# A two-layer graph network on one core: ACT fetches three of its edge tiles per sixteen bodies instead of one, between its scalings

## The reference, cut to what matters

```
hid    = silu(edge_scalars @ fc1)              # 10 or 64 inputs per edge
weight = hid @ fc2                             # 192 or 224 factors
row    = h[edge_src]                           # 160 numbers of the source node
msg    = weight * row, times parts of edge_attr (4 numbers)
agg    = segment_sum(msg, edge_dst)            # edges are sorted by destination
```

## Time and profile before

| | |
|---|---|
| median of 3 runs | 4053.01 us (4050.89 to 4054.45) |
| the profiled execution | 4054.16 us, its span 4052.2 us |
| PE busy | 3404.4 us (84%) |
| POOL busy | 2982.6 us (74%) |
| ACT busy | 2569.3 us (63%) |
| DVE busy | 2477.8 us (61%) |
| row fetches issued by SP / by ACT | 6208 / 1536 |
| granted clock of PE, mean | 0.99 |

### The profile page before, as it was taken

The page is one execution under the profiler, slowest core; times in us unless marked ns, Lnnn a source line. Parts: engine busy times, 40 slices in busy tenths (PEclk is TensorE's granted clock), DMA queues, the critical chain, the costliest instruction groups (busy, mean ns, idle before and its releaser), DMA issues. The chain is left out here.

```text
span 4052.2 us, 253752 instructions
## 1 busy us (share of the span) xinstructions
PE 3404.4 (84%) x91120; PEld 2590.9 (64%) x91121; DVE 2477.8 (61%) x7032; ACT 2569.3 (63%) x10506; POOL 2982.6 (74%) x3211
## 2 busy tenths in 40 slices
PE   8888888888887888888888888888888888888887
PEld 6666666666655665666776666666666666666666
DVE  6555555555545545445567777777776666666667
ACT  6666666666666666666466666666666666666665
POOL 5777777777777777777457777777777777777775
PEclk9999999999999999999999999999999999999999
DMA  5333333333333333333244444444443333333334
GB/s 158 86 86 88 86 88 88 87 86 86 81 75 76 78 75 76 77 76 76 84 130 112 109 112 109 109 112 110 111 113 100 97 100 100 97 100 99 97 100 122
DMA packets 357221, 390.23 MB, mean 96 GB/s; under 512 B 155141, under 2 KB 278825, under 8 KB 356646
## 3 DMA queue, kind: packets, MB, share of 16 engines
q0 software_dynamic: 147168, 251.36, 25.3%
q10 hardware_dynamic: 94848, 72.93, 6.7%
q1 hardware_dynamic: 114728, 61.70, 5.6%
HBM read 357.01 MB, written 23.76 MB: 94 GB/s over the span
## 5 line engine op out<-in xcount | busy, mean ns | idle before, releaser
L655 POOL DMA_INDIRECT e_rows<-scratch_table,k_index x3066 | 2899.7, 946 | 976.3 <-issue 831.3
L716 ACT ACTIVATE e_match<-e_match,e_attr 128x40 f32<-128x40 f32 x9408 | 2138.8, 315 | 36.5 <-issue 35.5
L773 PE MATMUL e_sum<-e_match,e_msg 128*32 128x40 f32 (+1 forms) x81536 | 1549.2, 215 | 513.4 <-DVE e_msg L986 248.0
L773 PEld LDWEIGHTS e_sum<-e_match,e_msg 128*32 128x32 f32 x81536 | 1340.1, 111 | 886.5 <-DVE e_msg L989 370.0
L980 DVE TENSOR_TENSOR e_msg<-e_w,e_rows 128x512 f32<-128x512 f32 x790 | 543.2, 688 | 1446.1 <-DMA e_rows<-scratch_table,k_index 1402.5
L707 ACT ACTIVATE e_hidden<-e_h 100x512 f32<-100x512 f32 (+1 forms) x784 | 384.2, 490 | 1329.4 <-PE e_h L755 1290.9
L766 PEld LDWEIGHTS e_w<-k_fc,e_hidden 100*128 100x128 f32 (+1 forms) x6272 | 808.7, 189 | 348.2 <-issue 330.2
L766 PE MATMUL e_w<-k_fc,e_hidden 100*128 100x192 f32 (+1 forms) x6272 | 1025.6, 366 | 0.6 <-issue 0.3
L755 PE MATMUL e_h<-e_inputs,k_fc 128*100 128x512 f32 (+1 forms) x1568 | 711.7, 536 | 105.0 <-issue 61.3
L986 DVE TENSOR_TENSOR e_msg<-e_w,e_rows 128x384 f32<-128x384 f32 x790 | 430.7, 545 | 0.3 <-issue 0.2
L983 DVE TENSOR_TENSOR e_msg<-e_w,e_rows 128x384 f32<-128x384 f32 x790 | 430.4, 545 | 0.0
(11 more groups left out here) (131 smaller groups left out, 1027.5 us busy)
## 6 DMA issues: line engine op xcount, KB each, us to landing
e_kept_rows<-scratch_table SPq DMA_DIRECT2D x6208, 0.6 KB
e_inputs<-in_inputs ACTq DMA_DIRECT2D x196, 256.0 KB
e_rows<-scratch_table,k_index POOLq DMA_INDIRECT x3066, 2.8
e_act_rows<-scratch_table ACTq DMA_DIRECT2D x1536, 0.6 KB
e_attr<-in_edge_attr ACTq DMA_DIRECT2D x390, 24.0 KB
e_inputs<-in_inputs ACTq DMA_DIRECT2D x196, 40.0 KB
e_xb<-in_xT SPq DMA_DIRECT2D x50, 128.0 KB
scratch_yT<-m_yT SPq DMA_DIRECT2D x10, 640.0 KB, 4.1
```

The source lines that it names most:

```text
L655: pool.indirect_dma_start(out=rows[j][:, t, :], out_offset=None, in_=table_dram, in_offset=bass.IndirectOffsetOnAxis(ap=index[k][:, c:c + ...
L716: last = nc.scalar.activation(match[j][:, t, c, :], match[j][:, t, 4, :], ACT.Copy, scale=attr[q][:, e0 + t, e:e + 1])
L773: return nc.tensor.matmul(out[32 * g:32 * g + 32, c0:c0 + n, :], m[:, f:f + 32], m5[:, which:which + n, :], start=first and opens, stop=en ...
```

## The change

ACT now fetches three tiles per span: group 2 at positions 5, 10 and 15. POOL leaves out the last tile of these three groups. SP's part stays as it is. ACT's 128 rows of a tile are spread evenly over the groups from the one two after the last placed tile to the one before the next (22, 18 and 18 groups), and within a group over four portions, one after the three scalings of each tile. A register load stands before every eighth row, wherever that falls. The copy into `rows` stands after the scalings of the group, and the load of the next node numbers right behind it.

```diff
--- before.py
+++ after.py
-FETCHED, FETCHED_GROUP, ACT_GROUP = (3, 7, 11, 15), 1, 2
+FETCHED, FETCHED_GROUP = (3, 7, 11, 15), 1
+ACT_FETCHED, ACT_GROUP = (5, 10, 15), 2
...
+def act_rows_due(position, j):
+
+    g = GPB * position + j
+    for k, at in enumerate(ACT_FETCHED):
+        first = GPB * ACT_FETCHED[k - 1] + ACT_GROUP + 2 if k else 0
+        count = GPB * at + ACT_GROUP - first
+        if first <= g < first + count:
+            return k, P * (g - first) // count, P * (g - first + 1) // count
+    return 0, 0, 0
...
-                fetched = started and (position in FETCHED and j == FETCHED_GROUP or position == SPAN - 1 and j == ACT_GROUP)
+                fetched = started and (position in FETCHED and j == FETCHED_GROUP or position in ACT_FETCHED and j == ACT_GROUP)
...
-            def row_numbers(span, batch):
+            def row_numbers(span, k, batch):
                 if batch == 0:
-                    landed, free = 16 * (span + 1), 16 * (FIRST + SPAN * span)
+                    landed = 16 * (len(ACT_FETCHED) * span + k + 1)
+                    free = 16 * (FIRST + SPAN * span + (ACT_FETCHED[k - 1] + 1 if k else 0))
...
-            def fetch_rows(batch, numbers, first, last):
-                for r in range(first, last):
-                    p = batch * BATCH + r
-                    act.dma_start(act_rows[p:p + 1, :], table_dram[bass.ds(numbers[r], 1), :]).then_inc(act_row_in, 16)
-
-            def place_rows(span):
-                landed, summed = 16 * P * (span + 1), GPB * (FIRST + SPAN * span + SPAN - 2) + ACT_GROUP + 1
+            def rows_between(span, position, j, loaded):
+
+
+                k, begin, end = act_rows_due(position, j)
+                shares = [range(begin + (end - begin) * t // TPG, begin + (end - begin) * (t + 1) // TPG) for t in range(TPG)]
+
+                def fetch(t):
+                    for p in shares[t]:
+                        if p % BATCH == 0:
+                            loaded[:] = row_numbers(span, k, p // BATCH)
+                        act.dma_start(act_rows[p:p + 1, :], table_dram[bass.ds(loaded[p % BATCH], 1), :]).then_inc(act_row_in, 16)
+                return fetch
+
+            def place_rows(span, k):
+                landed = 16 * P * (len(ACT_FETCHED) * span + k + 1)
+                summed = GPB * (FIRST + SPAN * span + ACT_FETCHED[k] - 1) + ACT_GROUP + 1
...
-                last.then_inc(scaled, 1)
+                    if t == TPG - 1:
+                        last.then_inc(scaled, 1)
+                    fetch(t)
...
                 for position in range(SPAN):
-                    each = BATCH // 2 if position == SPAN - 1 else BATCH // GPB
                     for j in range(GPB):
-                        places = position == SPAN - 1 and j == ACT_GROUP
-                        scale_matches(FIRST + SPAN * span + position, j, places)
-                        if j == 0:
-                            numbers = row_numbers(span, position)
-                        fetch_rows(position, numbers, min(j * each, BATCH), min(j * each + each, BATCH))
+                        places = position in ACT_FETCHED and j == ACT_GROUP
+                        fetch = rows_between(span, position, j, loaded)
+                        scale_matches(FIRST + SPAN * span + position, j, fetch, places)
                         if places:
-                            place_rows(span)
-                load_act_index(span + 1)
+                            k = ACT_FETCHED.index(position)
+                            place_rows(span, k)
+                            load_act_index(len(ACT_FETCHED) * span + k + 1)
```

More of the change, by code:

```diff
@@ L60 @@
 PER_BODY = 4
-FETCHED, FETCHED_GROUP, ACT_GROUP = (3, 7, 11, 15), 1, 2
+FETCHED, FETCHED_GROUP = (3, 7, 11, 15), 1
+ACT_FETCHED, ACT_GROUP = (5, 10, 15), 2
 PER_TILE = P // BATCH
 assert FIRST + SPAN * SPANS == BODIES and (NT - FIRST) % SPAN == 0 and SPAN == 4 * FETCHED[0] + 4
-assert PER_BODY * SPAN == len(FETCHED) * PER_TILE and SPAN == PER_TILE
+assert PER_BODY * SPAN == len(FETCHED) * PER_TILE and SPAN == ACT_FETCHED[-1] + 1
 FETCHED_TILES = SPANS * len(FETCHED)
@@ L70, in fetched_tile, with act_tile @@
     return ((FIRST + which * PER_BODY + PER_BODY - 1) * GPB + FETCHED_GROUP) * TPG + TPG - 1
-def act_tile(span):
-    return ((FIRST + span * SPAN + SPAN - 1) * GPB + ACT_GROUP) * TPG + TPG - 1
+ACT_TILES = SPANS * len(ACT_FETCHED)
+def act_tile(which):
+    span, k = divmod(which, len(ACT_FETCHED))
+    return ((FIRST + span * SPAN + ACT_FETCHED[k]) * GPB + ACT_GROUP) * TPG + TPG - 1
+def act_rows_due(position, j):
[6 more added lines that the diff above has]
+    return 0, 0, 0
 C_S, C_X = float(np.sin(np.pi / 8)), float(np.cos(np.pi / 8))
@@ L672, in _, with load_act_index @@
         def _(act):
-            def load_act_index(span):
-                act.dma_start(act_index[:, :], d["act_index"][:, bass.ds(span * BATCH, BATCH)]).then_inc(act_index_in, 16)
-            def row_numbers(span, batch):
+            def load_act_index(which):
+                act.dma_start(act_index[:, :], d["act_index"][:, bass.ds(which * BATCH, BATCH)]).then_inc(act_index_in, 16)
+            def row_numbers(span, k, batch):
                 if batch == 0:
-                    landed, free = 16 * (span + 1), 16 * (FIRST + SPAN * span)
+                    landed = 16 * (len(ACT_FETCHED) * span + k + 1)
+                    free = 16 * (FIRST + SPAN * span + (ACT_FETCHED[k - 1] + 1 if k else 0))
                     act.compute_val(landed)
@@ L701, in place_rows, with scale_matches @@
                 act.dma_start(rows[ACT_GROUP][:, TPG - 1, :], act_rows[:, :]).then_inc(act_placed, 16)
-            def scale_matches(i, j, places=False):
+            def scale_matches(i, j, fetch, places=False):
                 g, q, e0 = GPB * i + j, j // 2, (j % 2) * TPG
@@ L729, in _ @@
                 for j in range(GPB):
-                    scale_matches(i, j)
+                    scale_matches(i, j, lambda t: None)
             with act.Fori(0, SPANS) as span:
+                loaded = []
                 for position in range(SPAN):
-                    each = BATCH // 2 if position == SPAN - 1 else BATCH // GPB
                     for j in range(GPB):
-                        places = position == SPAN - 1 and j == ACT_GROUP
-                        scale_matches(FIRST + SPAN * span + position, j, places)
-                        if j == 0:
-                            numbers = row_numbers(span, position)
-                        fetch_rows(position, numbers, min(j * each, BATCH), min(j * each + each, BATCH))
+                        places = position in ACT_FETCHED and j == ACT_GROUP
+                        fetch = rows_between(span, position, j, loaded)
+                        scale_matches(FIRST + SPAN * span + position, j, fetch, places)
                         if places:
-                            place_rows(span)
-                load_act_index(span + 1)
-            act.wait_ge(act_index_in, 16 * (SPANS + 1))
+                            k = ACT_FETCHED.index(position)
+                            place_rows(span, k)
+                            load_act_index(len(ACT_FETCHED) * span + k + 1)
+            act.wait_ge(act_index_in, 16 * (ACT_TILES + 1))
             for q in range(2):
@@ L1359 @@
     ("src", (P, T + 2 * STEP), I32), ("dst_tile", (P, T), I32),
[L1360 removed]
+    ("row_index", (PER_TILE, (FETCHED_TILES + 2) * BATCH), I32), ("act_index", (PER_TILE, (ACT_TILES + 1) * BATCH), I32), ("dst_by_group", (GP, GQ, GE), I32),
     ("edge_attr", (P, T + STEP, 6), F32), ("inputs0", (NB0, EPAD + STEP * P), F32),
@@ L1439, in lay_out @@
     r["row_index"] = r["row_index"].reshape(PER_TILE, -1)
-    r["act_index"] = np.zeros((PER_TILE, SPANS + 1, BATCH), np.int32)
-    for span in range(SPANS):
-        r["act_index"][:, span] = by_tile[act_tile(span)]
+    r["act_index"] = np.zeros((PER_TILE, ACT_TILES + 1, BATCH), np.int32)
+    for which in range(ACT_TILES):
+        r["act_index"][:, which] = by_tile[act_tile(which)]
     r["act_index"] = r["act_index"].reshape(PER_TILE, -1)
```

## The result

The changed kernel takes 4023.52 us (median of 6 runs, 4019.09 to 4025.33), the kernel before 4052.39 us on the same chip (6 runs, 4050.89 to 4054.45): a ratio of 0.9927, 95% interval 0.9914 to 0.9939, 28.9 us less. The profiled execution took 4024.55 us, its span 4022.7 us.

What follows compares the result with a forecast made beforehand. POOL's back-to-back gather issue was taken to bind: 4054.2 us profiled, less 30.0 for 24 gathers, plus 1 for late chains, gives 4025.2; the runs' median lies 1.1 lower, so 4024 us, range 4020 to 4038.

Steps and rivals of the forecast that it cites:

- POOL's pace: POOL's gathers run back to back, 1.2506 us each; 24 fewer save 30.0 us, span 313.90 to 311.4 us.
- That POOL's issue time binds, and not the transfers: DMA engines are busy only 0.39 of the time; gathers come at POOL's own pace, 1.245 us each.
- ACT's part costs nothing: ACT's queue needs 282 us per span, 91% of POOL's 311.4, so its added fetches were taken as 0.
- Even there ACT's 4.8 just fits: In heavy stretches, ACT's 4.8 us per group fits within POOL's 4.86 to 4.93 us.
- The latency reserve: ACT's silu ahead of PE's next hidden product: ACT can be 3.2 us late before PE notices.
- The wait for the last row before the copy: ACT's place instruction waits 0 to 2.8 us for its last fetched row; nothing behind it is lost.
- SP falls behind but doesn't bind: With node terms SP needs 313.3 us per span, falling 1.9 us behind each; its index load has 8.8 us reserve.
- The late chains: SP's late placed tiles delay DVE, PE's sums and then POOL: 0 to 3 us together, 1 us in the sum.
- The first: SP's reserves are missing, so it binds in spans with node terms: 11 us come back, 4035 us; chance 0.12.
- The second: ACT overflows in heavy stretches as register loads wait for queued scalings: with four waited for, 4177 us; chance 0.09.
- Its point of decision: At 0.66 us of waiting per ACT register load, ACT's span reaches 314 us, the time of before.
- The third: No change: ACT and SP together eat the gain, about 4050 us; chance 0.05.

Runs made afterwards that it cites:

- POOL's part alone: Kernel before, with POOL skipping the two more gathers per span and nothing added to ACT (two tiles keep old rows): 4021.52 us, ratio 0.9927; slow chip 0.9948.
- ACT's part alone: Changed kernel, but POOL gathers all tiles as before; ACT fetches three tiles, copies only position 15's: 4050.76 us, ratio 0.9998; slow chip 1.0068.
- few register loads on ACT: Changed kernel, with ACT loading new row numbers only every fourth time, so rows of other edges are fetched: 4023.95 us, ratio 0.9930.
- four tiles: Changed kernel, with ACT fetching four tiles per span, group 2 at positions 3, 7, 11 and 15: 4680.3 us, ratio 1.1548.
- fewer register loads on SP: Changed kernel, with SP loading row numbers once per body instead of every eight rows, so rows of other edges are fetched: 4019.99 us, ratio 0.9921.
- the repeat of the changed kernel: Changed kernel with an unused SP register load that was absent from the program that ran, so the same kernel again: 4024.11 us, ratio 0.9927.
- fetches at the end: Changed kernel, with all of ACT's fetches of a group after its twelve scalings instead of in portions: 4021.03 us, ratio 0.9924; slow chip 1.0018.

## Why the prediction was right

**POOL's pace: right.** 24 gathers at 1.2506 us each were to give 30.0 us; POOL's part alone gave 30.3 us, the span of 16 bodies went to 311.43 us (311.4 predicted), and the 0.305 us before each gather stayed.

**That POOL's issue time binds, and not the transfers: right.** In the kernel with ACT's part alone 3072 rows more are fetched and the time is unchanged. In the one with POOL's part alone 24 gathers fewer give their full pitch. The sentence of the Trainium skill weighed in the prediction ("DMA: Bandwidth & Descriptors", section "Issuing engines are not separate DMA queues"), that the issuing engine's time is usually small beside the DMA, doesn't hold for these gathers: each takes 1.25 us of POOL's queue, where the page of the profile has a median of 2.9 us from issue to landing. A row costs 0.39 us of ACT's queue; its landing time is in no trace.

**ACT's part costs nothing: right, with two sizes off.** A fetch costs 0.39 us as predicted (1168.34 - 1167.95). The base of a group is 3.96 - 7 x 0.39 = 1.23 us, not 1.05. The load and its first fetch cost 5.02 - 3.96 = 1.06 us (1.09 predicted). A heavy group therefore takes 4.95 us on the mean of layer 0, (28 x 5.02 + 4 x 3.96 + 4 x 5.42) / 36, not 4.8; that is over PE's and POOL's 4.86 to 4.93. "Even there ACT's 4.8 just fits" was wrong by 0.15 us a group: ACT falls behind in each heavy stretch. With the light groups at 4.4 us and the empty ones at 3.1 us when ACT is late, it is 22 x 4.4 + 36 x 4.95 + 6 x 3.1 = 294 us per span, 94% of 311.4 instead of 91%.

**The latency reserve: right for PE, and not the last one.** Silu was to be late by at most 3.2 us before PE notices. Behind a heavy group it is late by 2.3 us in the median and 3.8 us at most in layer 0, by 2.8 and 4.2 us in layer 1, and PE does notice:

```profile
PE e_h L782 <- ACT e_hidden L733: 44.6, 58, 1.6
```

Ahead of these waits silu was 3.4 us late in the median. In the kernel before such waits are 1.2 us in all, and with few register loads on ACT as well, where the time is the same: so what PE waits for silu doesn't reach POOL. ACT works two groups ahead of DVE's messages, and those wait for POOL's rows (1206.4 us in all). In the light groups ACT gets back to its place: behind six fetches and a load its silu is late by 0.3 us in the median, against 2.3 behind the heavy ones. With four tiles the mean itself doesn't fit any more, and there the loss is 657 us.

**The wait for the last row before the copy: 0 to 0.6 us, at the lower end of 0 to 2.8 us.** A copy of a finished tile and the silu ahead of it, in ACT's timeline of layer 0:

```profile
1125.75 0.60 ACT L733 ACTIVATE e_hidden<-e_h 100x512 f32<-100x512 f32 x1 [1.66 <-PE e_h L782]
...
1126.91 0.50 ACTq L727 DMA_DIRECT2D e_rows<-e_act_rows  x1
```

This copy is issued 1.16 us after the silu, as all twelve of the kernel before are, so the rows were there. The 36 copies of the changed kernel stand 1.16 to 1.72 us behind their silu. DVE waited for a tile that ACT placed once in the whole trace, 1.3 us.

**SP falls behind but doesn't bind: right, and tighter than said.** SP's waits for gathers in all, and an index load with the gather that first uses it:

```profile
SPq L544 <- DMA e_rows<-scratch_table,k_index: 108.2, 55, 8.7
```

```profile
2718.57 0.38 SPq L545 DMA_DIRECT2D k_index<-in_src  x1
```

```profile
2727.53 0.95 POOL L671 DMA_INDIRECT e_rows<-scratch_table,k_index  x1 [0.30 <-issue]
```

In 2396 to 3020 SP doesn't wait for a gather once. Its index load stands 2718.57 - 2707.53 = 11.04 us behind the first gather of its span, where it was 7.19, and 8.96 us ahead of its use, where it was 12.8. SP's lag behind POOL grows by 3.45 us from the first span shown to the second, not by 1.9, and then no more (11.35 to 11.1 us behind the last gather of the body before). The margin held, 8.96 less 4.0 of landing.

**The late chains: 1.8 us where I took 1, and small terms beside them that I didn't have.** SP's tiles are late, not only the one at position 3 that I named: from position 15 of the first span shown to position 3 of the span behind the second, DVE waits for all six of them.

```profile
DVE e_msg L1007 <- DMA e_rows<-e_kept_rows: 25.1, 6, 5.8
```

The longest of these waits, at position 11 of the second of the two spans shown, all engines:

```profile
2937.61 0.51 SPq L587 DMA_DIRECT2D e_rows<-e_kept_rows  x1
...
2940.06 0.69 DVE L1007 TENSOR_TENSOR e_msg<-e_w,e_rows 128x512 f32<-128x512 f32 x1 [5.82 <-DMA e_rows<-e_kept_rows]
...
2946.28 0.64 PE L833 MATMUL e_sum<-k_node_s,e_xb 128*128 128x96 f32 x2
...
2947.72 0.94 POOL L671 DMA_INDIRECT e_rows<-scratch_table,k_index  x1 [0.93 <-PE e_sum L833]
```

DVE waits 5.82 us for the placed tile, PE's sums and the node term behind it come late, and POOL waits 0.93 us, 0.6 more than usual. The size: beyond the usual 0.305 us, POOL's seven long gaps add up to 5.4 us, the three of the kernel before to 2.4. Without these 3.0 us the edge phases would have become 30.2 us shorter instead of 27.2.

Of them 1.8 us lie in the four gaps from 2869.58 to 3045.70, in the stretch in which DVE waits for SP's tiles: these are the late chains, and with fewer register loads on SP all four are gone. In single traces of other kernels the same sum is 1.3 us (the repeat of the changed kernel), 0.7 (fetches at the end) and 2.4 (few loads on ACT). So the term lay inside the range of 0 to 3 us. POOL's part alone has no such gap, though SP lags there too (its index load in the same span stands 9.44 us behind the first gather, against 11.04): ACT's added rows seem to have a share in it, which no run isolates.

The other 1.2 us lie in the first 36 us of the layers, before any tile is placed, nearly all in one wait, shown here in the changed kernel and in the kernel before:

```profile
2084.87 0.96 POOL L671 DMA_INDIRECT e_rows<-scratch_table,k_index  x1 [2.41 <-PE e_sum L800]
```

```profile
2099.22 0.96 POOL L655 DMA_INDIRECT e_rows<-scratch_table,k_index  x1 [1.08 <-PE e_sum L773]
```

Over all traces with a granted clock of 0.98 to 0.99 this wait is 0.5 to 2.6 us, and 2.15 us in ACT's part alone, where POOL gathers as before; its cause stays open. The forecast had neither this nor the 2.3 us gained outside the edge phases, and that they nearly cancel is luck. All of it is as small as the 2 to 3 us by which runs of one kernel scatter about their median.

**The rivals.** The first (SP takes over, 4035 us) didn't come, but one register load more in every fourth body brings it, at 4035.23 us. That the two numbers agree is chance: the rival had all six spans with node terms at 313.3 us, and there three of layer 1 last 315.1, 316.9 and 313.7 us and one of layer 0 314.8. The second (a load that waits for the queued scalings) is refuted: the 576 loads between the scalings take 0.761 us in the median, the 192 behind them took 0.734. Its point of decision, 0.66 us per load, was 24 times the 0.027 us that were added, and a load with its first fetch still costs 1.06 us of ACT's queue. The profile does show what I had named as this rival's sign in the heavy groups (no wait for PE, 5.0 us from silu to silu), because my price of a heavy group was too low; the light groups make up for it. The third fell with the result.

The register loads of ACT in the changed kernel (times in ns: shortest, median, longest), and in the kernel before:

```profile
L701 ACTq TENSOR_LOAD <-k_act_index x576: 725/761/1152, 91.1 to 3942.5; - x192
```

```profile
L684 ACTq TENSOR_LOAD <-k_act_index x192: 724/734/746, 89.8 to 3963.5; - x192
```

**PE: right.** 85% busy over the span, 84% before.

## What to carry to other kernels

Work taken off the engine that issues back to back is worth its count times its pitch (busy time and the time between), here 24 x 1.25 us, if the queues that take it over have room: add up their issue times, register loads and dispatch per period, since their busy share (68% for ACT, whose queue was 94% full) doesn't show it. An engine may be late in every group of a stretch as long as its mean over the whole period fits and the buffers cover the peak; one tile beyond the mean cost 16%. Which engine is at the limit is a property of the chip as well: on the one where the kernel before takes 6618 us, the same work on ACT cost 42 us instead of nothing.

## What the hardware showed that I had not expected

- A load of eight numbers into registers between queued ACTIVATEs takes 0.76 us and doesn't wait for them to be executed; the next fetch takes 0.47 instead of 0.23 us.
- Between two chips the kernel before took 4052 and 6618 us. The granted clock of 0.83 instead of 0.99 doesn't explain it alone: PE's busy time went from 3404.4 to 4534.0 us (in the kernel with POOL's part alone), a factor 1.33, where the clock gives 1.19, and the span went up by 1.63. POOL's gathers took the same 0.945 us, and ACT was busy for 2569.0 us, as before (2569.3). What makes up the rest was not found.
- With four tiles for ACT the granted clock was 0.928, with SP's extra register load 0.978, against 0.989 in the changed kernel. What the lower clock adds to their losses was not measured.
